# Attention scores by pairs of heads in two row halves of TensorE, and GpSimd's weight subtraction moved behind the convolutions

## Time and profile before

| | us |
|---|---|
| median of 3 runs | 581.48 (579.0 to 583.66) |
| the profiled execution's own time | 584.92 |
| its span | 582.4 |
| PE busy | 514.3 (88%) |
| PEld busy | 486.5 (84%) |
| DVE busy | 371.0 (64%) |
| ACT busy | 350.7 (60%) |
| POOL busy | 289.1 (50%) |

### The profile page before, as it was taken

The page is one execution under the profiler, slowest core; times in us unless marked ns, Lnnn a source line. Parts: engine busy times, 40 slices in busy tenths (PEclk is TensorE's granted clock), DMA queues, the critical chain, the costliest instruction groups (busy, mean ns, idle before and its releaser), DMA issues.

```text
span 582.4 us, 13894 instructions
## 1 busy us (share of the span) xinstructions
PE 514.3 (88%) x4161; PEld 486.5 (84%) x4161; DVE 371.0 (64%) x1045; ACT 350.7 (60%) x743; POOL 289.1 (50%) x422
## 2 busy tenths in 40 slices
PE   3768989999999856769999999999999999999990
PEld 3656978878878655649999999999999999999990
DVE  1569778899899888813434447464645556666663
ACT  2456678788788555335555555657565666665551
POOL 0142525545535533054454454776776776754453
PEclk9769889999999965689999999999999999999996
DMA  8332062462362012110000000111111111100000
GB/s 217 126 108 74 1 169 59 111 168 68 101 168 71 3 48 38 12 25 21 20 17 20 22 16 20 34 35 38 34 34 39 36 34 38 34 19 20 20 29 27
DMA packets 49055, 31.68 MB, mean 54 GB/s; under 512 B 14203, under 2 KB 46662, under 8 KB 48998
## 3 DMA queue, kind: packets, MB, share of 16 engines
q1 hardware_dynamic: 44182, 21.77, 14.3%
q0 software_dynamic: 4096, 8.66, 5.5%
q10 hardware_dynamic: 720, 0.54, 0.3%
HBM read 22.25 MB, written 8.69 MB: 53 GB/s over the span
## 4 chain that ended last, share of the span: by engine, by line
PE 55%; DVE 4%; issue 1%; ACT 1%; DMA 0%; POOL 0%; DVEq 0%; ACTq 0%; POOLq 0%
PE ps L1569 25%; PE ps L1594 17%; PE ps L1584 9%; PE ps L1578 1%; PE ps L1427 1%; DMA xs<-rows_dram,idx 0%; DVE lohot L1257 0%; POOL out_dram L1530 0%; PE ps L1441 0%; PE ps L1406 0%; DVE hieq L1256 0%; DVE xs L1763 0%; ACT xs L1641 0%; DVE R L1227 0%; DVE hihot L1259 0%
## 5 line engine op out<-in xcount | busy, mean ns | idle before, releaser
L1569 PE MATMUL ps<-wts,xh 128*128 x620 | 155.3, 334 | 1.1 <-ACT xh L1658 1.1
L1752 DVE TENSOR_TENSOR h<-ps,sg 128x684 f32<-128x684 f32 x78 | 67.6, 866 | 91.7 <-PE ps L1569 79.8
L1547 POOL TENSOR_TENSOR xl<-xT,xh 127x128 fp32r<-127x128 f32 x155 | 68.1, 459 | 99.4 <-ACT xh L1658 96.1
L1594 PE MATMUL ps<-w2s,hT 115*128 (+1 forms) x930 | 116.5, 274 | 0.3 <-DVE xs L1763 0.3
L1594 PEld LDWEIGHTS ps<-w2s,hT 115*128 115x128 f32 (+1 forms) x930 | 109.9, 191 | 0.6 <-issue 0.6
L1569 PEld LDWEIGHTS ps<-wts,xh 128*128 128x128 f32 x620 | 105.4, 192 | 1.4 <-issue 1.3
L1569 PE MATMUL ps<-wts,xl 128*128 x310 | 99.9, 322 | 0.0
L1669 ACT ACTIVATE sg<-ps 128x684 f32<-128x684 f32 x78 | 57.6, 739 | 66.1 <-PE ps L1569 65.5
L1678 ACT ACTIVATE hT<-ps 114x768 f32<-114x768 f32 x78 | 62.9, 807 | 57.2 <-PE ps L1584 57.2
L1763 DVE SCALAR_TENSOR_TENSOR xs<-ps,xs 128x128 f32 x155 | 54.4, 351 | 52.5 <-PE ps L1594 37.1
L1530 POOL DMA_INDIRECT out_dram<-xs,idx x64 | 62.9, 982 | 26.2 <-issue 17.5
(11 more groups left out here) (282 smaller groups left out, 866.7 us busy)
## 6 DMA issues: line engine op xcount, KB each, us to landing
xt<-_attn_hidden_states_dram SPq DMA_DIRECT2D x8, 512.0 KB, 6.0
xres<-_attn_hidden_states_dram SPq DMA_DIRECT2D x7, 512.0 KB, 5.2
rows_dram<-x1s SPq DMA_DIRECT2D x7, 512.0 KB, 3.7
w2s<-in_L_ffn_W_dram SPq DMA_DIRECT2D x8, 171.0 KB
st<-in_L_ffn_Wg_dram SPq DMA_DIRECT2D x8, 171.0 KB, 3.1
st<-in_L_ffn_W_dram SPq DMA_DIRECT2D x8, 171.0 KB, 3.6
stl<-in_L_ffn_Wg_dram SPq DMA_DIRECT2D x8, 171.0 KB, 3.6
stl<-in_L_ffn_W_dram SPq DMA_DIRECT2D x8, 171.0 KB, 4.1
```

The costliest lines, as they stand in the source:

```text
L1547: v.tensor_tensor(xl[0:D - 1, i % 2, u, :], xT[0:D - 1, bass.ds(off[u], P)], xh[0:D - 1, i % 2, u, :].bitcast(F32), ALU.subtract).then_inc ...
L1569: mm = pe.matmul(ps[:, 2 * w + u, 0:HF], a[:, t % 2, u, :], wflat[:, bass.ds(w1[u] + (b + w * HF), HF)], start=(k == 0), stop=(k == 2))
L1594: mm = pe.matmul(ps[:, low(t) + u, 0:D], hT[0:n, t % 2, u, k, :], w2flat[0:n, bass.ds(w1[2 + u] + k * D, D)], start=(k == 0), stop=(k == 2))
L1752: v.tensor_tensor(h[:, t % 2, 0:units(t), :], ps[:, 2:2 + units(t), 0:HF], sg[:, 0:units(t), :], ALU.mult).then_inc(s["h_done"], 1)
```

## The change

1. The mask factors and their bf16 copies are doubled: what stood on partitions 0 to 15 stands on 64 to 79 as well.
2. Scores: a bank for each head h of a pair instead of each part i. Two mask products, one from the upper and one from the lower partitions; then for each part and each key head k (n = 0 to 7) and each h one product with 64 rows (partitions 64h on), 128 columns (two heads that share key head k, 64 queries each) and 64 keys moving. So 16 products in place of 32. `s_done` is raised for each bank at its last product, and these two stand last.
3. The first index of Sb, mx, sm and rs now means h; Pb is laid out as (part and key head, h, key) so that a turn reads 128 neighbours. GpSimd writes one h per product, with gaps. Each turn needs both GpSimd products, so TensorE waits for both.
4. o_w is loaded in one transfer in its own order; TensorE waits for `raw_in` 32.
5. GpSimd's second subtraction (L1013) stands behind the two probability products, and waits for `conv_done` of its step besides.

```diff
-    mq[q, np.arange(P)] = 1
+    mq[q, np.arange(P)] = mq[HD + q, np.arange(P)] = 1
...
-        mk[c, :, (c + 1) * LOW:] = -BIG
+        mk[c, :, (c + 1) * LOW:] = mk[HD + c, :, (c + 1) * LOW:] = -BIG
...
-        mqb = sb("mqb", [NC, P], BF16)
-        mkb = sb("mkb", [NC, 512], BF16)
+        mqb = sb("mqb", [HD + NC, P], BF16)
+        mkb = sb("mkb", [HD + NC, 512], BF16)
...
-        Pb = sb("Pb", [P, 2, NHP, LT])
+        Pb = sb("Pb", [P, NHP, 2, LT])
...
-            for h in range(2):
-                for a in range(2):
-                    sp.dma_start(owr[:, :, h, a, :], g["ow"].rearrange("o (k a h e) -> a h o k e", k=NKV, a=2, h=2)[a, h])\
-                      .then_inc(s["raw_in"], 16)
+            sp.dma_start(raw2, g["ow"]).then_inc(s["raw_in"], 16)
...
-            pe.wait_ge(s["raw_in"], 80)
+            pe.wait_ge(s["raw_in"], 32)
...
                     for i in range(2):
-                        pe.wait_ge(s["pn_done"], 2 * (t - 1) + i + 1)
+                        pe.wait_ge(s["pn_done"], 2 * t)
                         for k in range(NKV):
-                            mm = pe.transpose(ps[:, 2 + i, k * P:(k + 1) * P],
-                                              Pb[:, i, 2 * k:2 * k + 2, :].rearrange("p a k -> p (a k)"), ident)
+                            mm = pe.transpose(ps[:, 2 + i, k * P:(k + 1) * P], Pb[:, i * NKV + k, :, :].rearrange("p h k -> p (h k)"), ident)
...
-                    for i in range(2):
-                        pe.matmul(ps[:, 4 + i, :], mqb[:, :], mkb[:, :], start=True, stop=False)
-                        for n in range(NHP):
-                            for h in range(2):
-                                q0 = h * HD
-                                mm = pe.matmul(ps[q0:q0 + HD, 4 + i, n * LT:(n + 1) * LT], QB[q0:q0 + HD, i, n, :],
-                                               kT[q0:q0 + HD, n // 2, i, :], start=False, stop=(n == NHP - 1))
-                        mm.then_inc(s["s_done"], 1)
+                    for h in range(2):
+                        pe.matmul(ps[:, 4 + h, :], mqb[h * HD:h * HD + NC, :], mkb[h * HD:h * HD + NC, :], start=True, stop=False)
+                    for n in range(2 * NKV):
+                        i, k = n // NKV, n % NKV
+                        for h in range(2):
+                            mm = pe.matmul(ps[:, 4 + h, n * LT:(n + 1) * LT], QB[h * HD:(h + 1) * HD, i, 2 * k:2 * k + 2, :].rearrange("p n t -> p (n t)"),
+                                           kT[h * HD:(h + 1) * HD, k, i, :], start=False, stop=(n == 2 * NKV - 1))
+                            if n == 2 * NKV - 1:
+                                mm.then_inc(s["s_done"], 1)
...
+                    for i in range(2):
+                        pool.wait_ge(s["rec_done"], 2 * t + i + 1)
+                        if Y:
+                            pool.wait_ge(s["pt_done"], 2 * t)
+                        v.tensor_tensor(Pb[:, :, i, :], Sb[:, i, :, :], rs[:, i, :].unsqueeze(2).broadcast_to((P, NHP, LT)), ALU.mult).then_inc(s["pn_done"], 1)
+
+                    pool.wait_ge(s["conv_done"], 2 * t + 2)
                     pool.wait_ge(s["whi_done"], t + 1)
                     e = bass.ds(t, 1)
                     v.tensor_tensor(wts[:, e, 2 * HF:4 * HF].rearrange("p a h -> p (a h)"), st[:, 0:2 * HF],
                                     wts[:, e, 0:2 * HF].rearrange("p a h -> p (a h)").bitcast(F32), ALU.subtract).then_inc(s["wlo_done"], 1)
-                    for i in range(2):
-                        pool.wait_ge(s["rec_done"], 2 * t + i + 1)
-                        if Y:
-                            pool.wait_ge(s["pt_done"], 2 * t)
-                        v.tensor_tensor(Pb[:, i, :, :], Sb[:, i, :, :], rs[:, i, :].unsqueeze(2).broadcast_to((P, NHP, LT)), ALU.mult).then_inc(s["pn_done"], 1)
```

More of the change, by code:

```diff
@@ L325, in phase1 @@
         qr = raw.rearrange("p (j d) -> p j d", j=8)
-        owr = raw2.rearrange("p (k h a e) -> p k h a e", k=NKV, a=2, h=2)
         kvr = raw3.rearrange("p (j d) -> p j d", j=8)
@@ L552, in tail @@
                 for i in range(2):
-                    pe.wait_ge(s["pn_done"], 2 * (B - 1) + i + 1)
+                    pe.wait_ge(s["pn_done"], 2 * B)
                     for k in range(NKV):
-                        mm = pe.transpose(ps[:, 2 + i, k * P:(k + 1) * P], Pb[:, i, 2 * k:2 * k + 2, :].rearrange("p a k -> p (a k)"), ident)
+                        mm = pe.transpose(ps[:, 2 + i, k * P:(k + 1) * P], Pb[:, i * NKV + k, :, :].rearrange("p h k -> p (h k)"), ident)
                     mm.then_inc(s["pt_done"], 1)
@@ L792, in _ @@
             dve.wait_ge(s["const_in"], 32)
-            v.tensor_copy(mqb[:, :], mq[0:NC, :]).then_inc(s["prep_cst"], 1)
-            v.tensor_copy(mkb[:, :], mk[0:NC, :]).then_inc(s["prep_cst"], 1)
+            v.tensor_copy(mqb[:, :], mq[0:HD + NC, :]).then_inc(s["prep_cst"], 1)
+            v.tensor_copy(mkb[:, :], mk[0:HD + NC, :]).then_inc(s["prep_cst"], 1)
             dve.wait_ge(s["prep_al"], 2)
```

## The result

The changed kernel takes 577.64 us (median of 20 runs, 576.39 to 579.33), the kernel before 580.45 us (20 runs, 577.74 to 586.23). The ratio is 0.9956 with a 95% interval of 0.9941 to 0.997: 2.5 us faster, within 1% as forecast.

The account below looks back on a forecast made before the run. A TensorE and VectorE loop of 21.65 us was taken to bound the steady steps. Start -2.3, step 0 +0.1, step 1 +0.85 and +0.4, steps 3 to 7 -0.75: together -1.7, forecast 579.8 us, range 574 to 588.

Parts of the forecast that it names:

- What bounds the steps: Attention steps from step 3 on: one loop of TensorE 11.65, scores 1.51 and VectorE 8.49 us; 21.5 us afterwards.
- The tap: Third imaginary tap on VectorE falls from 1.68 to 0.64 us without GpSimd's subtraction beside it; row statistics stay unblocked.
- The scores: First maximum 2.40 us behind the mask instead of 1.51, +0.89 us a step; row halves overlap, 32 records in 1.89 us.
- The start: One o_w load lands 4.8 us behind its issue, so the first transpose starts near 7.2 us: -2.3 us.
- Both halves of the probabilities: TensorE's transposes wait for both GpSimd products: nothing in steady steps, +0.9 us at most in step 1, +0.4 taken.
- Step 1: Second attention step: first maximum at 52.63 instead of 51.78 us, +0.85 us, plus +0.4 for the transposes' wait.
- The weights' transfers: Subtraction's move delays the next weights' four loads on SP's queue; cost zero, landing 1.1 us before their GpSimd reader.
- The sum: Whole kernel: start, step 0, step 1 and steps 3 to 7 together give -1.7 us, step 2 adding 0.
- Rival (2): Score records stay at 0.036 us; VectorE's saving counts up to TensorE's 0.85 us idleness: -7.0 us, 574.5 us; chance 0.11.
- (1): Row halves of the scores don't overlap, 0.118 us a record, 3.78 us for the scores: +12.8, 594 us; chance 0.15.
- (4): Late weights or blocked row statistics in the steps, each 0.8 us a step: +3 in all, 584 us; chance 0.05.
- (3): A new TensorE idle stretch drops the granted clock in four of five steady steps: +5.1, 586.6 us; chance 0.08.

Follow-up runs that it names:

- experiment 1: Kernel before with o_w in one load alone, q_w's turned blocks written in the other order to match: 577.95 us, ratio 0.9988.
- experiment 8: Kernel before with one o_w load, subtraction moved, and the gate's mean product ahead of the second x1s turns: 570.31 us, ratio 0.985.
- experiment 2: Kernel before with only GpSimd's second subtraction moved behind the probability products and conv_done: 575.56 us, ratio 0.9935.
- experiment 3: Kernel before with one o_w load and the subtraction moved, scores as before: 572.64 us, ratio 0.9877.
- experiment 4: Changed kernel with the subtraction back in its old place and o_w in four loads, so new scores alone: 581.35 us, ratio 1.0024.
- experiment 7: Changed kernel with VectorE's third tap (tap 2) ahead of the first maximum: 576.2 us, ratio 0.9946.
- experiment 5: Changed kernel with all score products of one row half ahead of those of the other: 580.97 us, ratio 1.000.

## Why the prediction held, and where its terms were off

The forecast was 1.7 us below the median shown; the medians differ by 2.8 us, the ratio says 2.5. By its own steps:

- **What bounds the steps.** Right. The loop 11.65 + 1.51 + 8.49 us became 11.66 + 2.35 + 7.44 = 21.45 us (111.71, 114.06, 121.50 and 133.16). Forecast 21.5.
- **The tap.** Right: 1.04 us gone, statistics not blocked. The lock of the Trainium skill (SBUF — State Buffer, "Who interferes with whom") agrees with the runs on both sides, taps 2.52 us and statistics 1.65 us beside the same subtraction.
- **The scores.** Right in mechanism and size up to the first maximum: +0.84 us for +0.89, with a record at 0.0625 us for 0.059. The second mask costs only 0.01 us more for both (0.39 for the pair, 0.38 for one), where I took 0.15. A single row half needs 0.106 us a record, close to the router's 0.118: so halving the rows saved next to nothing, and alternating between two halves saved the rest. Both rules of the Trainium skill that were weighed (TensorE: Matmul & The Clock Gate, "LDWEIGHTS (loading the stationary operand)" and TensorEngine Tiling (Array Packing), "Key Properties") hold here, the first at 0.106 and the second at 0.0625.
- **The start.** -2.3 forecast, -2.04 in the profile (-2.22 in experiment 1), and that they are so near is luck. The load itself gave 1.18 us: the first turns came at 8.35 us, not near 7.2, because the one load landed 7.0 us behind its issue and not 4.8 like q_w's. The constants' cast starts at 7.80 instead of 6.83, so these loads probably share time with the new one. The other 0.86 us is the pace of the turns, which differs between executions with the same load: with one load the centroids' products came at 13.96 to 15.06 us in six kernels (16.11 in experiment 8, whose first turns came at 9.37), with four loads at 15.90 to 16.35 in three.
- **Both halves of the probabilities.** Mis-sized. Step 0 and 1 meet at the turns: in the kernel after all eight start 9.78 us behind the mask, and the transform starts 11.54 us behind it. With the old scores (experiment 1) the second four start at 9.71 and the transform at 10.62. So scores against subtraction cancel to +0.07 (forecast +0.1), and the wait for both halves costs 0.85 us, the bound of 0.9 and not the 0.4 I took. Against the profile of before 0.35 us of it came back when the clock returned (5.26 us from the transform to the queries, 5.61 before), which makes the row of step 0, +0.57 for +0.5. That is luck too. In experiments 1, 2, 3 and 8, with the old scores, the same stretch took 4.03 to 4.81 us, in the five kernels with the new ones 5.16 to 5.54: there the clock came back later, and step 0 as a whole took 23.66 to 23.95 us against 21.80 to 22.14. So the new form costs step 0 up to 2 us, and I had counted on the clock to give something back. Why it came back later isn't shown.
- **Step 1.** +0.85 forecast, and it is there in step 1: 21.25 us after, 20.41 in experiment 1. But step 2 takes it back, and steps 1 and 2 together are 42.58 against 42.52 us. In both kernels SP issues the xres load 2.05 us behind step 2's mask; in experiment 1 it landed 7.0 us later and VectorE waited 0.61 us for it, in the kernel after it landed 5.2 us later and VectorE didn't wait at all. The prediction had the wait and took it as fixed. Why the load was quicker isn't shown.

```profile
74.72 1.28 DVE L911 SCALAR_TENSOR_TENSOR xres<-xres,ps 128x512 f32<-128x512 f32 x2 [0.61 <-DMA xres<-_attn_hidden_states_dram]
```

```profile
77.19 1.28 DVE L909 SCALAR_TENSOR_TENSOR xres<-xres,ps 128x512 f32<-128x512 f32 x2
```

(The first is experiment 1, the second the kernel after, both in step 2.)

- **The weights' transfers.** The cover held in the steady steps: last issue at 126.01, reader at 131.50, with no wait for the load. In step 1 the first subtraction did wait for its load until 42.71 us, one of the signs named for being wrong, and then held six real taps (5.29 us for 4.04), which TensorE's work there hides.
- **The sum.** Against the profile of before the traces give -2.0 (start), +0.6 (step 0), +0.1 (steps 1 and 2) and 5 x -0.2: -2.3 us, with -2.5 by the ratio. The terms missed by +0.3, +0.1, -0.7 and -0.25 us, so errors cancelled in part. With step 0 as the other kernels with the old scores show it the same sum is about -1 us. How step 0 goes in a usual execution of before isn't known, since only one was profiled, so the traces support the forecast's size and not its single terms at the start and in step 0.
- **Terms that don't add.** The prediction wrote a steady step as +0.89 - 1.04. That is right for both edits together and wrong for each of them:

| steady step, us | subtraction in its old place | moved |
|---|---|---|
| old scores | 21.65 | 20.78 |
| new scores | 21.63 | 21.45 |

Alone, the scores cost nothing in a steady step (experiment 4) and the move gives 0.87, cut off by TensorE; on top of the other, the scores cost 0.67 and the move gives 0.18. Step 0 shows the same up to the turns, which start 9.72 us behind the mask before, 9.76 with the new scores alone, 9.28 with the move alone and 9.78 with both. Rival (2) used the limit of 0.85, so the piece was known. What I did not do was to ask it of each part, and my expectation for experiment 4 (22.4 us) failed on it.
- **The rivals.** (1) is refuted: 2.00 us for the records, not 3.78. (2) is refuted: 0.0625, not 0.036. (4) did not occur in the steady steps. (3) did not occur in the kernel after: 1.33 us of idleness in each step left the clock at 1.00. The granted clock did matter, but in the profiled execution of before: its fall ahead of steps 2 and 3 is the largest part of the spans' difference. That execution had a mean granted clock of 0.934, while 27 of the 29 others of the same kernel in the first set had 0.941 to 0.948; so the 3.4 us by which it stood above the median are probably this in part, which I had not seen. Only in part, since others of these 29 took 582.83 and 583.87 us at 0.943 and 0.942.

What stays open: what sets the clock's falls and returns (below), and whether what the new scores cost beside the moved subtraction (0.67 us in a steady step, 1.89 in step 0, 23.95 against 22.06 in experiment 3) could be won back by an order that gives VectorE other work; experiment 7 won 0.39 us a step of it.

## What to carry to other kernels

Before adding up the terms of a change with several parts, ask for each part alone what closes the loop with and without the others: two costs that wait for the same instruction count once, and a saving ends where the next engine has no idle time left. Before a single profile is read term by term, compare its stretches with those of other executions: here step 0 of the kernel before took 1.2 to 1.6 us longer than in four kernels with the same scores. Halving the rows of these small products hardly made them quicker; what helped is that products in separate row halves alternate, and even then fewer and wider products can be slower than many narrow ones in four quarters. If a GpSimd instruction that reads SBUF must run beside VectorE, put it beside instructions that read one tile.

## What the runs showed of the hardware

- Float32 records with 64 keys moving, 64 rows and 128 columns of weights: 0.106 us each in one row half (32 in 3.39 us), 0.0625 us alternating between the halves (32 in 2.00 us). With 64 rows and 64 columns in two quarters of the array a record of the old form takes 0.036 us (32 in 1.15 us). So a pair of heads costs 0.125 us as one wide product (two records) and 0.144 us as two narrow ones (four records): the new form is 13% less, and from the mask product to the x1s turns TensorE needs 2.25 us (111.71 to 113.96) instead of 2.79 (130.80 to 133.59 in experiment 2). Beside the moved subtraction it still loses, since both banks end together and the first is complete 0.84 us later.
- Two bf16 mask products from separate row halves into separate banks take 0.39 us together, one takes 0.38.
- Idle time alone did not decide the granted clock. Ahead of the turns behind step 1 TensorE idled 2.48 us in the kernel before and 2.53 us in the kernel after; the first ran on at 0.50, the second at 1.00. In experiment 1 the same 2.48 us of idleness was followed by turns of 1.09 us, at 1.00 (54.04). The rows of before and after:

```profile
58.99 1.97 PE L441 MATMUL ps<-cr,Pb 128*128 128x128 f32 x8 [2.48 <-DVE xres L913]
```

```profile
57.30 1.06 PE L436 MATMUL ps<-cr,Pb 128*128 128x128 f32 x8 [2.53 <-DVE xres L909]
```

- Early in the launch eight turns take 1.94 us, as long as at a granted clock of 0.50 (1.93 and 1.97 us), and the third group in the kernel after 1.08, as at 1.00 (1.09), though the profile's column gives 1.00 from 8 to 14 us throughout. With one o_w load this group took from 1.08 (experiment 1) to 1.90 us (experiment 7), with TensorE busy from the first turn to the last.
- In experiment 5 the clock fell to 0.50 in steps 2, 5 and 7, just behind 3.39 us of records in one row half at a time, with TensorE busy throughout, and in steps 3, 4 and 6 with the same order it did not. From 96 to 176 us it stayed at 1.00 in all the other kernels, the kernels before and after among them.
